# A mixture-of-experts kernel: the norms of the experts' gate and down weights taken by VectorE's maxima instead of TensorE's Gram products

## Chip, cores and metric

The kernel runs on one core of one Trainium2 chip. The metric is the device time of one execution in microseconds (us); lower is better. The median of three executions of the kernel before is 210.87 us (210.85 to 211.42).

## What is computed

For 32 sequences of 128 rows of 128 numbers, the reference adds a shared gated MLP and two of eight expert MLPs, chosen per sequence, to the input:

```
def _gemma_mlp(x, gate_w, up_w, down_w):
    g = jnp.einsum('bsh,hi->bsi', x, gate_w)
    u = jnp.einsum('bsh,hi->bsi', x, up_w)
    return jnp.einsum('bsi,ih->bsh', jax.nn.gelu(g, approximate=True) * u, down_w)
w, sel = jax.lax.top_k(softmax(router_logits), 2)
w = w / w.sum(axis=-1, keepdims=True)
...
out = out + _gemma_mlp(x, shared_gate, shared_up, shared_down)
x = x + out
```

The hidden width is 512. The weights of one kind of all eight experts are 128 x 4096 floats (2 MB).

## The kernel before

**Number format.** Only the first group of sequences is multiplied in fp32. Everything else is split: an operand is scaled by a power of two and written as a float16 high part and a float16 low part, and a product is three float16 matmuls (high by high, high by low, low by high). Each operand needs a bound of its size before it can be scaled. For x and for the shared weights VectorE takes the largest magnitude of each partition (`tops`, L379), squares it (`mask`, L393), TensorE adds the squares over the partitions with a matrix of ones (`spread_norms`, L585 and L586), and VectorE turns the exponent into scales (`scales`, L408 to L412). For the experts' weights (kinds K_GATE, K_UP and K_DOWN) TensorE multiplies each 128 x 128 block of the weights, read as bf16, with itself and adds up all 32 blocks of a kind in one PSUM tile (`gram`, L576); VectorE then keeps the diagonal (`mask`, L397), TensorE spreads it (L588), and VectorE takes the largest of it (L406) ahead of the same scales.

**Steps.** The work is 96 steps. Steps 0 to 31 are the shared MLP (8 groups of 4 sequences by 4 blocks of 128 hidden units), steps 32 to 95 the experts (32 sequences by 2). Within step t of the shared part TensorE computes the gate block G(t) (L612 to L614, output g_ps), the down block D(t - lag) of an earlier step (L625 to L627, o_ps), then the up block U(t) (L612 to L614, u_ps). The lag is 3 up to step 11, 4 up to 17, 5 up to 23, then 6; at a step where it grows there is no down block. ScalarE takes the gelu of G(t) (L335). VectorE multiplies it with U(t) into the hidden tile; this product is called H(t) below (L457). ScalarE casts H(t) to its float16 high part (L340), and GpSimd subtracts the high part from H(t) for the low part (L304), called LO(t) below. D(t) needs LO(t). G(t) and U(t) reuse two PSUM buffers each, so U(t) waits until H(t - 2) is done:

```
pe.wait_ge(gelu_ok if q == GATE else h_ok, t - 1)
```

**Side work by tables.** Every engine runs its own program in order, and tables that are keyed by step place the side work between the steps. `TOP_AT` places the maxima of x, `MASK_AT`, `SPREAD_AT` the two halves of each norm, `X_AT` the splits of x (ScalarE's high part L344, then VectorE's low part `x_low`, L418, one step later), `PIECES` the splits of the expert weights in 12 pieces of two experts (ScalarE L349, then VectorE `skill_low`, L424, one step later), `K_STEPS` the steps from which TensorE takes the Gram blocks, four steps of eight matmuls for each kind. At a step in `X_AT` or `PIECES`, GpSimd starts LO(t) only when VectorE's low part of that split is done. Group 7's first gate block, at step 28, waits for the split of x that is placed at step 23. `add_group` (L468) adds a finished group of outputs on VectorE. At the step `SKILL_TABLES_AT` GpSimd computes the scales for the expert steps, which G(32)'s gelu and H(32) wait for. Within a step VectorE's order is: H(t), `x_low` or `skill_low` of the step before, the maxima, `scales`, `mask`, `add_group`.

The Gram batch of the down weights starts with a wait for the diagonal of the up weights, since both use one PSUM tile:

```
if n == 0 and kind:
    pe.wait_ge(diag_ok, K_OF[kind - 1] + 1)
```

Of the kernel before, what the change touches and what calls it, by code (L numbers as in the profile page):

```python
# [5 lines left out]
ALU = mybir.AluOpType  # L6
ACT = mybir.ActivationFunctionType
AX = mybir.AxisListType
F32 = mybir.dt.float32
# [5 lines left out]
P = 128  # L15
# [13 lines left out]
def build(nc, xT, cond, skills, shared, outT):  # L29
    B, E = cond.shape  # L30
# [3 lines left out]
    I = W // 3  # L34
    C = I // P
    GR = 512 // S
    G = B // GR
    GN = GR * S
    assert H == P and S == P and I == GN and C == 4 and G == 8 and E == 8
    GATE, UP, DOWN = 0, 1, 2  # L40
# [7 lines left out]
    XF, XA = 2, 5  # L48
# [3 lines left out]
    with ctx:  # L52
        def sb(name, shape, dt):
            return ctx.enter_context(nc.sbuf_tensor(name, shape, dt))
# [4 lines left out]
        def sem(name):  # L59
            return ctx.enter_context(nc.semaphore(name))  # L60
# [5 lines left out]
        wsk32 = sb("wsk32", [P, 3 * E * I], F32)  # L66
# [4 lines left out]
        zeros = sb("zeros", [P, GN], BF16)  # L71
        ones = sb("ones", [P, P], BF16)
        ident = sb("ident", [P, P], F32)
        floor = sb("floor", [P, 3 + XF], BF16)
        diag = sb("diag", [P, P], BF16)


        DC, GC, UC, XC, KC = 0, 1, 2, 3, 3 + G
# [60 lines left out]
        r_wexp = sem("r_wexp")  # L139
        r_words = sem("r_words")  # L140
        top_ok = sem("top_ok")
        gram_ok = sem("gram_ok")
        diag_ok = sem("diag_ok")
        norm_ok = sem("norm_ok")
# [27 lines left out]

        FIRST, X_NEXT, K_GATE, X_REST, K_UP, K_DOWN = range(6)
        K_OF = (K_GATE, K_UP, K_DOWN)
        COLS = [(DC, XC + XF), (XC + XF, XC + XA), (KC, KC + 1), (XC + XA, XC + G), (KC + 1, KC + 2), (KC + 2, KC + 3)]


# [3 lines left out]


        TOP_AT = {1: (2,), 3: (3, 4), 10: (5,), 11: (6,), 12: (7,)}
        TOP_OF = {FIRST: 3 + XF, X_NEXT: 3 + XA, X_REST: 3 + G}
        K_STEPS = [5, 10, 15]
        MASK_AT = {3: X_NEXT, 9: K_GATE, 12: X_REST, 14: K_UP, 19: K_DOWN}
        SPREAD_AT = {4: X_NEXT, 11: K_GATE, 14: X_REST, 16: K_UP, 21: K_DOWN}
        ROUTE_AT = 6
        ROUTED_AT = 11

        TABLE_AT = {4: X_NEXT, 15: X_REST}
        SKILL_TABLES_AT = 23


        X_AT = {3: 0, 5: 2, 8: 3, 11: 4, 15: 5, 19: 6, 23: 7}
        X_NTH = {1: 1} | {j: n + 2 for n, j in enumerate(X_AT.values())}
        EG = 2
        PIECES = {12 + 2 * n: n for n in range(3 * E // EG)}


        def lag(t):
# [175 lines left out]
        def _(dve):  # L377
# [7 lines left out]
            def top_x(j):  # L385
                dve.wait_ge(x_in[0 if j == 0 else 1 if j < XF else 2 if j < XA else 3], 16)
                tops(XC + j, xT32[:, j * GN:(j + 1) * GN])

            def mask(n):
                a, b = COLS[n]  # L390
                if n not in K_OF:
                    dve.wait_ge(top_ok, TOP_OF[n])
                    nc.vector.tensor_tensor(top2[:, a:b], top[:, a:b], top[:, a:b], ALU.mult).then_inc(diag_ok, 1)  # L393
                else:
                    kind = K_OF.index(n)
                    dve.wait_ge(gram_ok, kind + 1)
                    nc.vector.scalar_tensor_tensor(out=diag[:, :], in0=n_ps[0][:, 0:P], scalar=NORM_FLOOR,  # L397
                                                   in1=ident[:, :], op0=ALU.add, op1=ALU.mult).then_inc(diag_ok, 1)

            def scales(n):  # L400
                a, b = COLS[n]
                dve.wait_ge(norm_ok, n + 1)
                norm = n_ps[1][:, 0:b - a]
                if n in K_OF:
                    norm = n_all[:, a:b]
                    nc.vector.tensor_reduce(norm, n_ps[1][:, 0:P], AX.X, ALU.max).then_inc(n_red, 1)  # L406
                    dve.wait_ge(n_red, K_OF.index(n) + 1)
                nc.vector.tensor_scalar(e_bits[:, a:b], norm.bitcast(U32), 1, EXP_MASK,  # L408
                                        ALU.logical_shift_right, ALU.bitwise_and).then_inc(s_step, 1)
                dve.wait_ge(s_step, n + 1)  # L410
                nc.vector.tensor_scalar(i_bits[:, a:b], e_bits[:, a:b], 1.0, INV_FIELD * ONE_EXP, ALU.mult, ALU.add)
                nc.vector.tensor_scalar(s_bits[:, a:b], e_bits[:, a:b], -1.0, SCALE_FIELD * ONE_EXP,  # L412
                                        ALU.mult, ALU.add).then_inc(scaled, 1)
                dve.wait_ge(scaled, n + 1)
# [111 lines left out]
            for t in range(STEPS):  # L526
                hidden(t)

                if t - 1 in X_AT:
                    x_low(X_AT[t - 1])  # L530
                if t - 1 in PIECES:
                    skill_low(PIECES[t - 1])
                if t == 0:
                    scales(FIRST)
                if t in TOP_AT:
                    for j in TOP_AT[t]:
                        top_x(j)
                if t == 2:
                    shared_low(GATE, 1)
                    x_low(1)  # L540
                    shared_low(UP, 2)
                if t == C:
                    shared_low(DOWN, 3)
                if t in SPREAD_AT:
                    scales(SPREAD_AT[t])
                if t in MASK_AT:
                    mask(MASK_AT[t])
                if t == C - 1:
                    routing_weights()
                    routing_spread()  # L550
                if t == ROUTED_AT:
                    routed_tables()

                if t == 7:
                    add_group(0)
                n, c = divmod(down_of(t - 1), C)
                if c == C - 1 and 1 <= n < G and down_of(t - 1) != down_of(t - 2):
                    add_group(n)
                b, k = divmod(t - SH - LAG - 1, TOP_K)
                if k == TOP_K - 1 and b >= 0:  # L560
                    add_row(b)
# [4 lines left out]
        def _(pe):  # L566
# [4 lines left out]
            def gram(out, src, start):  # L571

                n = src.shape[1] // P
                for i in range(n):
                    block_ap = high_bits(src[:, i * P:(i + 1) * P])
                    last = nc.tensor.matmul(out, block_ap, block_ap, start=(start and i == 0), stop=(i == n - 1),  # L576
                                            skip_group_check=True)
                return last

            def spread_norms(n):  # L580
                a, b = COLS[n]
                pe.wait_ge(diag_ok, n + 1)
                if n not in K_OF:
                    sums = n_ps[1][:, 0:b - a]
                    nc.tensor.matmul(sums, ones[:, :], floor[:, 0:b - a], start=True, stop=False)  # L585
                    nc.tensor.matmul(sums, ones[:, :], top2[:, a:b], start=False, stop=True).then_inc(norm_ok, 1)  # L586
                else:
                    nc.tensor.matmul(n_ps[1][:, 0:P], ones[:, :], diag[:, :], start=True, stop=True).then_inc(norm_ok, 1)  # L588
# [95 lines left out]
            for t in range(2, SH):  # L684
                if t >= C:
                    half_shared(t, GATE)
                    if down_of(t) >= C and down_of(t) != down_of(t - 1):
                        down_shared(down_of(t))

                    if t - C < 2:  # L690
                        down_first(t - 2)
                    if t in SPREAD_AT:
                        spread_norms(SPREAD_AT[t])
                    half_shared(t, UP)
                elif t == C - 1:
                    gate_up_first(t, GATE)
                    gate_up_first(t, UP)
                    down_first(1)
                for kind in range(3):
                    n = t - K_STEPS[kind]  # L700
                    if 0 <= n < 4:
                        if n == 0:
                            pe.wait_ge(sk_in[kind], 16)
                        if n == 0 and kind:
                            pe.wait_ge(diag_ok, K_OF[kind - 1] + 1)
                        a = (kind * E + 2 * n) * I
                        for half in range(2):
                            last = gram(n_ps[0][:, 0:P], wsk32[:, a + half * I:a + (half + 1) * I],
                                        n == 0 and half == 0)
                        if n == 3:  # L710
                            last.then_inc(gram_ok, 1)
                if t == ROUTE_AT:
                    pe.wait_ge(r_spread, 2 * TOP_K)
                    pe.wait_ge(s_step, X_NEXT + 1)
                    nc.tensor.matmul(n_ps[1][:, P:P + 2 * TOP_K * B], ones32[:, :], spread[:, :, :].rearrange("p b q -> p (b q)"),
                                     start=True, stop=True).then_inc(r_routed, 1)
# [73 lines left out]
```

## Time and profile before

| | |
|---|---|
| median of three executions | 210.87 us |
| the profiled execution, its own time | 211.93 us |
| its span in the trace | 210.1 us |
| granted TensorE clock | full in every stretch |
| TensorE busy | 205.2 us of the span |
| VectorE, ScalarE, GpSimd busy | 123.6, 133.8, 117.9 us |

The span is the time from the first to the last instruction in the trace. The profiled execution's own time is 1.8 us longer than its span, and 1.06 us longer than the median of the three. The work of each engine is read from a list of its instructions in order of time; an instruction of a row starts when the one ahead of it on that engine lets it, which for VectorE is a little before the recorded end of that one.

### The profile page before, as it was taken

The numbers are of one execution on the slowest core, as the hardware profiler recorded it, in microseconds if no ns is written. First come the engines' busy times: TensorE is split into PE (matmuls) and PEld (weight loads), VectorE is DVE, ScalarE is ACT, GpSimd is POOL, SyncE is SP. The second block draws the span as 40 slices with busy tenths as digits, with TensorE's granted clock in tenths as the row PEclk, the third lists the DMA queues.
The fourth block names the chain that finished last, engine by engine and source line by source line (L and its number), as shares of the span: only waits on it lengthen the run. The fifth ranks groups of instructions, "written<-read, shape, count | busy, mean of one in ns | idle before, by whom it ended". The sixth has DMA issues, their size and how long they took to land.

```text
span 210.1 us, 6672 instructions
## 1 busy us (share of the span) xinstructions
PE 205.2 (98%) x2695; PEld 165.0 (79%) x2695; DVE 123.6 (59%) x217; ACT 133.8 (64%) x217; POOL 117.9 (56%) x129
## 2 busy tenths in 40 slices
PE   7999999989999999999999999999999999999995
PEld 2444555445444478899999999999999999999995
DVE  2899657977999988554353444434435435344452
ACT  6283767677989997655656656556565565655650
POOL 3023644359548997665565655655656556565562
PEclk9999999999999999999999999999999999999999
DMA  6999600000000000000010010010010010010011
GB/s 196 391 433 434 296 2 0 0 3 0 2 0 5 0 0 3 0 3 5 3 53 3 0 53 3 3 53 0 3 55 3 3 53 0 3 53 4 3 50 53
DMA packets 2813, 11.70 MB, mean 56 GB/s; under 512 B 352, under 2 KB 608, under 8 KB 2400
## 3 DMA queue, kind: packets, MB, share of 16 engines
q1 hardware_dynamic: 2640, 11.01, 13.1%
q8 instruction: 23, 0.38, 0.7%
q10 hardware_dynamic: 144, 0.26, 0.7%
q14 instruction: 6, 0.05, 0.1%
HBM read 9.18 MB, written 2.10 MB: 54 GB/s over the span
## 4 chain that ended last, share of the span: by engine, by line
PE 93%; DVE 4%; issue 1%; ACT 0%; POOL 0%; POOLq 0%
PE o_ps L664 7%; PE g_ps L646 7%; PE u_ps L646 7%; PE o_ps L663 7%; PE u_ps L645 7%; PE g_ps L645 7%; PE u_ps L644 7%; PE g_ps L644 7%; PE o_ps L662 7%; PE u_ps L612 3%; PE g_ps L612 3%; PE g_ps L614 2%; PE o_ps L627 2%; PE o_ps L625 2%; PE o_ps L626 2%; PE g_ps L613 2%
## 5 line engine op out<-in xcount | busy, mean ns | idle before, releaser
L304 POOL TENSOR_TENSOR h<-h 128x512 f16<-128x512 f32 x92 | 109.2, 1194 | 79.2 <-ACT h L340 57.9
L457 DVE SCALAR_TENSOR_TENSOR h<-gel,sk_factor,u_ps 128x512 f32<-128x512 f32 x64 | 47.8, 747 | 68.0 <-PE u_ps L646 39.0
L335 ACT ACTIVATE gel<-g_ps,sk_gate 128x512 f32<-128x512 f32 x64 | 43.9, 687 | 49.8 <-PE g_ps L646 49.8
L340 ACT CAST h<-h 128x512 f16<-128x512 f32 x92 | 56.0, 609 | 3.5 <-DVE h L457 3.5
L645 PE MATMUL g_ps<-x,wsk 128*128 128x128 f16 x256 | 46.2, 219 | 0.0
L646 PE MATMUL g_ps<-x,wsk 128*128 128x128 f16 x256 | 46.2, 219 | 0.0
L645 PE MATMUL u_ps<-x,wsk 128*128 128x128 f16 x256 | 46.2, 219 | 0.0
L646 PE MATMUL u_ps<-x,wsk 128*128 128x128 f16 x256 | 46.2, 219 | 0.0
L644 PE MATMUL u_ps<-x,wsk 128*128 128x128 f16 x256 | 46.2, 219 | 0.0
L644 PE MATMUL g_ps<-x,wsk 128*128 128x128 f16 x256 | 46.2, 219 | 0.0
L663 PE MATMUL o_ps<-h,wsk 128*128 128x128 f16 x256 | 45.9, 219 | 0.0
L664 PE MATMUL o_ps<-h,wsk 128*128 128x128 f16 x256 | 45.9, 219 | 0.0
L662 PE MATMUL o_ps<-h,wsk 128*128 128x128 f16 x256 | 45.9, 219 | 0.0
L457 DVE SCALAR_TENSOR_TENSOR h<-gel,sh_factor,u_ps 128x512 f32<-128x512 f32 x28 | 20.7, 741 | 8.6 <-ACT gel L335 4.3
L645 PEld LDWEIGHTS u_ps<-x,wsk 128*128 x256 | 25.0, 98 | 0.7
L644 PEld LDWEIGHTS u_ps<-x,wsk 128*128 x256 | 25.1, 98 | 0.7
L335 ACT ACTIVATE gel<-g_ps,sh_gate 128x512 f32<-128x512 f32 x28 | 19.1, 681 | 10.1 <-PE g_ps L614 9.9
L645 PEld LDWEIGHTS g_ps<-x,wsk 128*128 x256 | 25.0, 98 | 0.1
L644 PEld LDWEIGHTS g_ps<-x,wsk 128*128 x256 | 25.0, 98 | 0.1
L646 PEld LDWEIGHTS g_ps<-x,wsk 128*128 x256 | 25.1, 98 | 0.0
L664 PEld LDWEIGHTS o_ps<-h,wsk 128*128 x256 | 25.0, 98 | 0.0
L646 PEld LDWEIGHTS u_ps<-x,wsk 128*128 x256 | 25.0, 98 | 0.0
(103 smaller groups left out, 310.1 us busy)
## 6 DMA issues: line engine op xcount, KB each, us to landing
wsk<-skills SPq DMA_DIRECT2D x3, 2048.0 KB, 16.1
outT<-xT SPq DMA_DIRECT2D x7, 256.0 KB, 2.0
xT<-xT SPq DMA_DIRECT2D x2, 768.0 KB, 6.3
wsh<-shared SPq DMA_DIRECT2D x3, 256.0 KB, 3.9
xT<-xT ACTq DMA_DIRECT2D x1, 256.0 KB, 3.5
xT<-xT SPq DMA_DIRECT2D x1, 256.0 KB, 4.6
outT<-xT SPq DMA_DIRECT2D x1, 192.0 KB, 2.6
outT<-xT SPq DMA_DIRECT2D x1, 64.0 KB, 1.5
```

What stands on the lines that cost most here:

```text
L304: nc.gpsimd.tensor_tensor(hidden_lo(t), hidden_full(t), hidden_hi(t), ALU.subtract).then_inc(lo_ok, 1)
L335: nc.scalar.activation(gel[:, t % NG, :], g_ps[t % 2][:, :], ACT.Gelu_apprx_tanh, scale=scale).then_inc(gelu_ok, 1)
L340: nc.scalar.copy(hidden_hi(t), hidden_full(t)).then_inc(hi_ok, 1)
L457: nc.vector.scalar_tensor_tensor(out=h32[:, t % N32, :], in0=gel[:, t % NG, :], scalar=factor, in1=u_ps[t % 2][:, :], op0=ALU.mult, op1=AL ...
L612: nc.tensor.matmul(out, w_hi, xh, start=True, stop=False)
L613: nc.tensor.matmul(out, w_hi, xl, start=False, stop=False)
L644: nc.tensor.matmul(cols, w_hi[c], xh, start=True, stop=False)
L645: nc.tensor.matmul(cols, w_hi[c], xl, start=False, stop=False)
L646: last = nc.tensor.matmul(cols, w_lo[c], xh, start=False, stop=True)
L662: nc.tensor.matmul(out, w_hi[c], hi, start=(k == 0 and c == 0), stop=False)
L663: nc.tensor.matmul(out, w_hi[c], lo, start=False, stop=False)
L664: last = nc.tensor.matmul(out, w_lo[c], hi, start=False, stop=(k == TOP_K - 1 and c == C - 1))
```

## The change

The Gram product stays for the up weights alone (`GRAMS`) and runs at steps 9 to 12 instead of 10 to 13. For the gate and the down weights VectorE takes the largest magnitude of each partition over two experts at a time (`part_top`: 128 x 1024 floats to 128 x 1), four times for each kind, at steps 5, 6, 7, 8 and 17, 19, 21, 23. It then reduces the four to one and goes the way of x: square, sum over the partitions with the matrix of ones, scales. The tables move: gate's norm is ready a step earlier, down's 6 steps later; the splits of the last four groups of x come one step later; the splits of the gate and up weights come one step earlier; those of the down weights stay where they were; GpSimd's tables for the experts come at step 28 instead of 23.

```
+        GRAMS = (K_UP,)
...
-        TOP_OF = {FIRST: 3 + XF, X_NEXT: 3 + XA, X_REST: 3 + G}
-        K_STEPS = [5, 10, 15]
-        MASK_AT = {3: X_NEXT, 9: K_GATE, 12: X_REST, 14: K_UP, 19: K_DOWN}
-        SPREAD_AT = {4: X_NEXT, 11: K_GATE, 14: X_REST, 16: K_UP, 21: K_DOWN}
+        TOP_OF = {FIRST: 3 + XF, X_NEXT: 3 + XA, X_REST: 4 + G, K_GATE: 4 + XA, K_DOWN: 5 + G}
+        PART_AT = {5: (GATE, 0), 6: (GATE, 1), 7: (GATE, 2), 8: (GATE, 3), 17: (DOWN, 0), 19: (DOWN, 1), 21: (DOWN, 2), 23: (DOWN, 3)}
+        K_STEPS = {K_UP: 9}
+        MASK_AT = {3: X_NEXT, 8: K_GATE, 12: X_REST, 14: K_UP, 24: K_DOWN}
+        SPREAD_AT = {4: X_NEXT, 10: K_GATE, 14: X_REST, 16: K_UP, 27: K_DOWN}
...
-        SKILL_TABLES_AT = 23
-        X_AT = {3: 0, 5: 2, 8: 3, 11: 4, 15: 5, 19: 6, 23: 7}
+        SKILL_TABLES_AT = 28
+        X_AT = {3: 0, 5: 2, 8: 3, 12: 4, 16: 5, 20: 6, 24: 7}
...
-        PIECES = {12 + 2 * n: n for n in range(3 * E // EG)}
+        PIECES = {t: n for n, t in enumerate((11, 13, 15, 17, 19, 21, 23, 25, 28, 30, 32, 34))}
...
+            def part_top(kind, n):
+                if n == 0:
+                    dve.wait_ge(sk_in[kind], 16)
+                nc.vector.tensor_reduce(parts[:, kind // 2, n:n + 1], wsk32[:, (kind * E + 2 * n) * I:(kind * E + 2 * n + 2) * I],
+                                        AX.X, ALU.max, apply_absolute_value=True).then_inc(part_ok, 1)
+
             def mask(n):
                 a, b = COLS[n]
-                if n not in K_OF:
+                if n in K_OF and n not in GRAMS:
+                    kind = K_OF.index(n)
+                    dve.wait_ge(part_ok, E // 2 if kind == GATE else E)
+                    tops(KC + kind, parts[:, kind // 2, :])
+                if n not in GRAMS:
                     dve.wait_ge(top_ok, TOP_OF[n])
                     nc.vector.tensor_tensor(top2[:, a:b], top[:, a:b], top[:, a:b], ALU.mult).then_inc(diag_ok, 1)
...
+                if t in PART_AT:
+                    part_top(*PART_AT[t])
...
-                if n not in K_OF:
+                if n not in GRAMS:
                     sums = n_ps[1][:, 0:b - a]
...
-                for kind in range(3):
-                    n = t - K_STEPS[kind]
+                for batch in GRAMS:
+                    kind = K_OF.index(batch)
+                    n = t - K_STEPS[batch]
...
-                        if n == 0 and kind:
-                            pe.wait_ge(diag_ok, K_OF[kind - 1] + 1)
```

TensorE around steps 5 to 7, before (output and inputs by name; g_ps0 and u_ps0 belong to even steps):

```order
L614 MATMUL u_ps1<-x2,wsh 128x512
L576 MATMUL n_ps0<-wsk32 128x128 x8
L612 MATMUL g_ps0<-x2,wsh 128x512
L613 MATMUL g_ps0<-x2,wsh 128x512
L614 MATMUL g_ps0<-x2,wsh 128x512
L612 MATMUL u_ps0<-x2,wsh 128x512
L613 MATMUL u_ps0<-x2,wsh 128x512
L614 MATMUL u_ps0<-x2,wsh 128x512
L576 MATMUL n_ps0<-wsk32 128x128 x8
L715 MATMUL n_ps1<-spread,ones32 128x128
```

and with the change, the same place:

```order
L629 MATMUL u_ps1<-x2,wsh 128x512
L627 MATMUL g_ps0<-x2,wsh 128x512
L628 MATMUL g_ps0<-x2,wsh 128x512
L629 MATMUL g_ps0<-x2,wsh 128x512
L627 MATMUL u_ps0<-x2,wsh 128x512
L628 MATMUL u_ps0<-x2,wsh 128x512
L629 MATMUL u_ps0<-x2,wsh 128x512
L728 MATMUL n_ps1<-spread,ones32 128x128
```

The eight Gram matmuls of each step are gone here, and so at seven other places, less the up batch, which moves one step forward.

VectorE from H(23) to H(27), before (h32 is the hidden tile, wsk a weight split, x2 a split of x, xT32 an added group):

```order
L457 SCALAR_TENSOR_TENSOR h32<-gel,sh_factor,u_ps1 128x512
L424 SCALAR_TENSOR_TENSOR wsk<-wsk32,s_bits,wsk 128x1024
L457 SCALAR_TENSOR_TENSOR h32<-gel,sh_factor,u_ps0 128x512
L418 SCALAR_TENSOR_TENSOR x2<-xT32,s_bits,x2 128x4x128
L457 SCALAR_TENSOR_TENSOR h32<-gel,sh_factor,u_ps1 128x512
L424 SCALAR_TENSOR_TENSOR wsk<-wsk32,s_bits,wsk 128x1024
L457 SCALAR_TENSOR_TENSOR h32<-gel,sh_factor,u_ps0 128x512
L468 SCALAR_TENSOR_TENSOR xT32<-o_ps0,sh_inv,xT32 128x512
L457 SCALAR_TENSOR_TENSOR h32<-gel,sh_factor,u_ps1 128x512
```

and with the change, the same five products:

```order
L470 SCALAR_TENSOR_TENSOR h32<-gel,sh_factor,u_ps1 128x512
L396 TENSOR_REDUCE parts<-wsk32 128x1
L470 SCALAR_TENSOR_TENSOR h32<-gel,sh_factor,u_ps0 128x512
L437 SCALAR_TENSOR_TENSOR wsk<-wsk32,s_bits,wsk 128x1024
L383 TENSOR_REDUCE top<-parts 128x1
L407 TENSOR_TENSOR top2<-top 128x1
L470 SCALAR_TENSOR_TENSOR h32<-gel,sh_factor,u_ps1 128x512
L431 SCALAR_TENSOR_TENSOR x2<-xT32,s_bits,x2 128x4x128
L470 SCALAR_TENSOR_TENSOR h32<-gel,sh_factor,u_ps0 128x512
L437 SCALAR_TENSOR_TENSOR wsk<-wsk32,s_bits,wsk 128x1024
L481 SCALAR_TENSOR_TENSOR xT32<-o_ps0,sh_inv,xT32 128x512
L470 SCALAR_TENSOR_TENSOR h32<-gel,sh_factor,u_ps1 128x512
```

A maximum over two experts and down's first half of the norm have come in, each weight split stands a step earlier, and the split of x a step later.

## Rows read from the trace of the kernel before

**Rows 1.** The page: busy time; the chain that ended last.
```profile
PE 205.2 (98%) x2695; PEld 165.0 (79%) x2695; DVE 123.6 (59%) x217; ACT 133.8 (64%) x217; POOL 117.9 (56%) x129
...
PE 93%; DVE 4%; issue 1%; ACT 0%; POOL 0%; POOLq 0%
```

**Rows 2.** Windows: us, then busy us and instruction count per engine, granted clock, DMA.
```profile
20.88:36.83 15.95, 15.95 (x111) 8.59 (x110) 10.40 (x22) 11.34 (x19) 7.95 (x10) 1.00 0.24 103
36.83:48.72 11.89, 10.72 (x76) 5.59 (x74) 10.67 (x21) 8.61 (x13) 5.78 (x6) 1.00 0.01 1
48.72:60.05 11.33, 11.33 (x61) 5.40 (x59) 9.87 (x17) 9.98 (x15) 7.70 (x10) 1.00 0.00 1
60.05:72.09 12.04, 12.04 (x57) 5.30 (x56) 11.21 (x14) 10.86 (x17) 9.35 (x12) 1.00 0.01 2
```

**Rows 3.** TensorE in order of time: start, us, work, idle before it.
```profile
31.85 0.38 PE L625 MATMUL o_ps<-h,wsh 128*128 128x512 f16 x1
...
34.95 0.62 PE L576 MATMUL n_ps<-wsk 128*128 128x128 bf16 x8
35.42 0.38 PE L612 MATMUL g_ps<-x,wsh 128*128 128x512 f16 x1
...
39.60 0.18 PE L585 MATMUL n_ps<-floor,ones 128*128 128x3 bf16 x1 [0.33 <-DVE top L393]
...
43.26 0.62 PE L576 MATMUL n_ps<-wsk 128*128 128x128 bf16 x8 [0.84 <-DVE diag L397]
...
60.84 0.39 PE L612 MATMUL u_ps<-x,wsh 128*128 128x512 f16 x1
...
67.33 0.38 PE L612 MATMUL g_ps<-x,wsh 128*128 128x512 f16 x1
...
70.57 0.38 PE L612 MATMUL u_ps<-x,wsh 128*128 128x512 f16 x1
```

**Rows 4.** VectorE in order of time, same columns.
```profile
14.83 1.27 DVE L379 TENSOR_REDUCE top<-xT 128x1 f32<-128x512 f32 x2
...
20.88 0.75 DVE L457 SCALAR_TENSOR_TENSOR h<-gel,sh_factor,u_ps 128x512 f32<-128x512 f32 x1
...
29.66 0.75 DVE L418 SCALAR_TENSOR_TENSOR x<-xT,s_bits,x 128x512 f16<-128x512 f32 x1
...
33.46 0.75 DVE L457 SCALAR_TENSOR_TENSOR h<-gel,sh_factor,u_ps 128x512 f32<-128x512 f32 x1 [1.18 <-ACT gel L335]
34.12 0.68 DVE L379 TENSOR_REDUCE top<-xT 128x1 f32<-128x512 f32 x1
...
40.12 1.27 DVE L424 SCALAR_TENSOR_TENSOR wsk<-wsk,s_bits 128x1024 f16<-128x1024 f32 x1
41.32 0.73 DVE L457 SCALAR_TENSOR_TENSOR h<-gel,sh_factor,u_ps 128x512 f32<-128x512 f32 x1
41.98 0.15 DVE L408 TENSOR_SCALAR e_bits<-n_ps 128x3 uint32<-128x3 uint32 x1
42.16 0.56 DVE L411 TENSOR_SCALAR i_bits<-e_bits 128x3 int32<-128x3 uint32 x1
...
45.97 0.75 DVE L457 SCALAR_TENSOR_TENSOR h<-gel,sh_factor,u_ps 128x512 f32<-128x512 f32 x1 [1.01 <-ACT gel L335]
...
60.05 1.40 DVE L457 SCALAR_TENSOR_TENSOR h<-gel,sh_factor,u_ps 128x512 f32<-128x512 f32 x2
...
68.11 0.73 DVE L457 SCALAR_TENSOR_TENSOR h<-gel,sh_factor,u_ps 128x512 f32<-128x512 f32 x1
68.77 2.17 DVE L424 SCALAR_TENSOR_TENSOR wsk<-wsk,s_bits 128x1024 f16<-128x1024 f32 x1
```

**Rows 5.** GpSimd in order of time, same columns.
```profile
30.55 2.27 POOL L304 TENSOR_TENSOR h<-h 128x512 f16<-128x512 f32 x2 [2.83 <-DVE x L418]
33.32 1.16 POOL L304 TENSOR_TENSOR h<-h 128x512 f16<-128x512 f32 x1 [0.50 <-ACT h L340]
...
41.54 2.27 POOL L304 TENSOR_TENSOR h<-h 128x512 f16<-128x512 f32 x2 [2.02 <-DVE wsk L424]
...
65.78 1.24 POOL L284 TENSOR_SCALAR tmp_k<-s_bits 128x8 f32<-128x8 f32 x1
...
68.70 11.94 POOL L304 TENSOR_TENSOR h<-h 128x512 f16<-128x512 f32 x8
```

More of the change, by code:

```diff
@@ L73, in build @@
         ident = sb("ident", [P, P], F32)
+        parts = sb("parts", [P, 2, E // 2], F32)
         floor = sb("floor", [P, 3 + XF], BF16)
@@ L141, in build @@
         top_ok = sem("top_ok")
+        part_ok = sem("part_ok")
         gram_ok = sem("gram_ok")
@@ L394, in mask @@
                 else:
-                    kind = K_OF.index(n)
-                    dve.wait_ge(gram_ok, kind + 1)
+                    dve.wait_ge(gram_ok, GRAMS.index(n) + 1)
                     nc.vector.scalar_tensor_tensor(out=diag[:, :], in0=n_ps[0][:, 0:P], scalar=NORM_FLOOR,
@@ L403, in scales @@
                 norm = n_ps[1][:, 0:b - a]
-                if n in K_OF:
+                if n in GRAMS:
                     norm = n_all[:, a:b]
                     nc.vector.tensor_reduce(norm, n_ps[1][:, 0:P], AX.X, ALU.max).then_inc(n_red, 1)
-                    dve.wait_ge(n_red, K_OF.index(n) + 1)
+                    dve.wait_ge(n_red, GRAMS.index(n) + 1)
                 nc.vector.tensor_scalar(e_bits[:, a:b], norm.bitcast(U32), 1, EXP_MASK,
@@ L703, in _ @@
                             pe.wait_ge(sk_in[kind], 16)
-                        if n == 0 and kind:
-                            pe.wait_ge(diag_ok, K_OF[kind - 1] + 1)
                         a = (kind * E + 2 * n) * I
                         for half in range(2):
-                            last = gram(n_ps[0][:, 0:P], wsk32[:, a + half * I:a + (half + 1) * I],
-                                        n == 0 and half == 0)
+                            last = gram(n_ps[0][:, 0:P], wsk32[:, a + half * I:a + (half + 1) * I], n == 0 and half == 0)
                         if n == 3:
```

## The prediction

> **What bounds the kernel now.** I read the page first. TensorE is busy 205.2 us of a 210.1 us span, and 93% of the chain that ended last is TensorE's own instructions [rows 1]. That says little about this change, because it moves work only between about 20 and 75 us, and the other engines are near their limit there. So the windows come second: VectorE is busy for 10.40 of 15.95 us from H(5) to H(12), 10.67 of 11.89 us from H(12) to H(17), 9.87 of 11.33 us up to H(22), and 11.21 of 12.04 us up to H(29) [rows 2]. TensorE is busy throughout except in the second window, where it stands for 0.33 us and 0.84 us, both times for VectorE [rows 3]. The reader should see two engines almost level. Freeing TensorE brings time only as far as VectorE, which gets the work, lets it run ahead.
>
> A difference under 0.3%, 0.63 us, is one that a measurement of this kernel can't tell from none.
>
> **What TensorE loses.** A group of eight Gram matmuls takes 0.47 us, from 34.95 to the gate block at 35.42 [rows 3]. Eight such groups go, four of the gate weights and four of the down weights: 8 x 0.47 = 3.8 us. The wait of 0.84 us at 43.26 [rows 3] goes with the down batch. The two small matmuls that spread a diagonal become pairs of as small ones, nothing. If TensorE alone decided, the span would fall by 3.8 + 0.84 = 4.6 us.
>
> **What VectorE gains.** No row shows a maximum over 1024 floats. The nearest rows bound it. Two maxima over 512 end 1.27 us after the first starts, one alone is 0.68 us, so one starts 0.59 to 0.60 us after another [rows 4]. Twice that, 1.20 us, is the upper bound. For the lower one: a split of 1024 floats takes 1.20 us from start to start (40.12 to 41.32) and a product over 512 takes 0.66 us (41.32 to 41.98) [rows 4], so 512 floats more cost 0.54 us and the rest is fixed: 0.60 + 0.54 = 1.14 us. Both kinds run on the same engine, so I take 1.13 us, at the lower bound. Eight make 9.0 us. The small instructions (reduce four values, square) are worth what leaves (diagonal, largest of it), 0.4 us either way.
>
> **The port.** Some VectorE instructions stop for a running GpSimd one: the split at 68.77 takes 2.17 us instead of 1.27, beside a GpSimd subtraction that starts at 68.70 [rows 4, 5], and the small scale instruction at 42.16 takes 0.56 us, until the first of two GpSimd subtractions that start at 41.54 is over [rows 4, 5]. The price is up to what is left of one subtraction, 2.27 / 2 = 1.14 us. Products and maxima aren't hit: the maximum at 34.12 takes 0.68 us beside the subtraction that starts at 33.32 [rows 4, 5]. So the eight new maxima wait for nobody. The Trainium skill ("SBUF — State Buffer", Who interferes with whom) says the same of tensor_reduce on this chip, and that of two instructions that contend the one that issues second is blocked for the whole of the other. If maxima did contend, the four of the down weights could each cost up to 1.14 us more, 4.6 us in all, and the sum below would be 5.3 instead of 0.7; the trace speaks against that.
>
> **Walk through the steps.** VectorE's row starts at 20.88 for H(5), as before. Every chain of VectorE's below takes 0.66 us for a product, an x split or an added group.
>
> *Steps 5 to 11.* Five products, two groups of other 0.66 us (x split, added group), four maxima at 1.13 and gate's first half, 0.45 us, are 3.30 + 1.32 + 4.52 + 0.45 = 9.6 us, so the split of group 3 starts at 30.5 instead of 29.66 [rows 4]. VectorE stood idle here for much of the time (10.40 of 15.95 us busy [rows 2]); that cover is used up. LO(8) is held for this split: before it started at 30.55, 0.89 us after the split's start, and the down block that needs it at 31.85 [rows 3, 5]. Now it starts at 31.3 and takes 1.14 us, and the down block starts at about 32.6. TensorE, which did 1.9 us less Gram work in steps 5 to 8 but 0.47 us more at step 9, is 0.7 us late, and H(11) starts at 34.15 instead of 33.46 [rows 4].
>
> *Steps 11 to 16.* The first two weight splits come here in both kernels. The square of x's maxima at step 12 runs into LO(11), 0.65 us, and the second split into LO(12), 0.6 us. But TensorE has no wait of 0.84 us and no Gram work at steps 13, 15 and 16. VectorE's chain reaches the up diagonal at 44.1, U(16) follows at 44.5 and H(16) at 45.4 instead of 45.97 [rows 4]: now 0.6 us early.
>
> *Steps 16 to 22.* VectorE is the bound. Before, this stretch took 60.05 - 45.97 = 14.1 us [rows 4], with some 1.2 us of it idle. Three maxima come in (3.4 us), the down norm leaves (0.95 us), and port waits stay about as long: 14.1 - 1.2 + 3.4 - 0.95 - 0.6 (product by product) = 14.75 us. H(22) starts at 60.15 instead of 60.05. U(24) needs it: it started 0.79 us after H(22), at 60.84 [rows 3], and now starts at 60.95. By that step TensorE has nothing left of its gain: it stands there for 2 us.
>
> *Steps 22 to 27.* H(22) to H(26), 3.3 us; three weight splits where there were two, since they stand a step earlier, 3.6; the x split, 0.66; the last maximum, 1.13; the down norm's first half, 0.4; the added group, 0.66; port waits for x split and third weight split, 0.65. Sum 10.4 us, against 68.11 - 60.05 = 8.06 [rows 4]. H(27) starts at 70.5 instead of 68.11. U(29) needs it 0.79 us later, at 71.3; before it ran at 70.57 and had 1.7 us of slack [rows 3]. That is **+0.7 us**. The x split of group 7, a step later, ends at 67.6 and lets G(28) start at 67.75 instead of 67.33 [rows 3]: +0.4, inside the other.
>
> *After step 27.* VectorE is free of maxima, TensorE runs on its own work as before, and nothing gives the 0.7 us back. GpSimd's tables for the experts take 2.9 us (65.78 to 68.70 [rows 5]). They come after LO(28), which waits for the first down split, at about 75, so end near 79. The gelu of step 32 would want them at about 77.3. U(34) and G(34) are what wait for it, two steps of 2 us on, so I cost the move at nothing.
>
> Sum: -4.6 us of TensorE's, of which nothing is left at step 24, and +0.7 us of VectorE's at step 29. On the profiled execution's 211.93 us that gives 212.6 us; its time stands 1.06 us above the median of 210.87, so the median becomes **211.6 us**.
>
> **Rivals.** *The port falls worse at step 14.* The scales of x's last groups follow the second weight split directly, and LO(13) is held for that same split. Before, a product lay between (41.32 [rows 4]). If GpSimd starts first, the scale instruction waits the 1.14 us. It delays the up diagonal, which TensorE waits for in front of U(16), and everything behind. VectorE's instruction would come about 0.03 us earlier by the pace of the rows, too close to call. Price +1.1: median 212.7. The Trainium skill ("SBUF — State Buffer", Who interferes with whom) says that the order of issue alone decides which of the two is blocked.
>
> *TensorE keeps a part of its gain (faster).* The place is the x split of group 7 in front of G(28), and H(27) behind it. My walk has port waits of 1.25 us between H(11) and H(16) and 0.65 us from there to that split. If 1.15 us of these 1.9 don't fall, and as much before H(27), G(28) starts at 66.6 instead of 67.33 and U(29) with it: -0.7 us, median 210.15. It starts to be faster at all from 0.42 us less of VectorE time ahead of that split, and can be measured from 1.05 us less. For it speaks that my port waits are estimates from the overlap of two engines whose phase shifts; against it, that a wait of 0.9 us for the port did fall in the kernel before (68.77 [rows 4]).
>
> *GpSimd late.* If LO(28) and the tables slip beyond about 80.5, gelu(32) holds G(34), and the expert steps start late: for each us that the chain is later than in my walk, up to one us. With the 11.94 us of eight subtractions in a row [rows 5] GpSimd had hardly any slack in that stretch. Price +2: median 212.9 to 213.5.
>
> *The change not doing what it says* is out: the order of instructions shows the Gram groups gone and the maxima in place. The data moved are the same, and the norm's value changes no duration.
>
> **How the numbers follow.** My case has a chance of 0.42, with an own range of 210.7 to 212.3 (maxima of 1.20 instead of 1.13 add 0.3, port waits of half or one and a half times my count -0.6 or +0.6); of it 0.02 lies under -0.63 us, 0.18 within, 0.22 above. The port at step 14 has 0.25, all slower. The faster rival has 0.20, of which 0.16 is faster and 0.04 within. GpSimd late has 0.07, slower. A cancelling of these effects near zero has 0.06. Together: faster 0.18, same 0.28, slower 0.54. The range for 8 in 10 reaches from the faster rival's 210.0 to the late tables' 213.1.
>
> **What would show it.** Right: the maxima at 1.13 to 1.20 us; H(11) at about 34.2, U(16) at 44.5, a wait of TensorE of some 2 us for H(22) in front of U(24), H(27) at 70.5, and TensorE without a wait from step 30 on. Wrong: TensorE waits of under 1 us in all between 45 and 72 us, or H(27) before 69.7, which would make it faster; a wait of a gelu for GpSimd's tables that reaches TensorE.

## The result and the profile after

The changed kernel takes 214.37 us (median of four, 213.95 to 214.71) against 210.90 us before: a ratio of **1.0151, 95% interval 1.0132 to 1.0171**. The forecast was slower by 0.7 us, 211.6 us, in a range of 210.0 to 213.1 us. The kernel is slower by 3.2 us by the ratio (3.5 us between the two medians), and its time lies outside that range. The direction was right, the size was not. In the three later series the kernel before had medians of 211.5 to 211.7 us, so a part of the gap may be that its first four executions were short ones.

The spans of the two profiled executions differ by only 2.1 us (212.2 and 210.1). The start hides a part of the difference: up to H(5), where both programs still do the same, the execution before took 20.88 us and the one after 20.04 us, since the first transfers and matmuls fall a little differently in each execution (19.66 to 21.50 us over all kernels of this study). So I compare from the start of H(5) to the start of VectorE's last instruction. Before that is 207.82 - 20.88 = 186.94 us, after it is 209.85 - 20.04 = 189.81 us: **+2.87 us**. Below, "length" means this number, and a time behind a plus sign is measured from H(5).

The page of the changed kernel, busy time of the engines, answers to [rows 1]:

```profile
PE 201.9 (95%) x2633; PEld 160.3 (76%) x2633; DVE 131.3 (62%) x225; ACT 133.9 (63%) x217; POOL 114.5 (54%) x129
```

TensorE is busy 3.3 us less and VectorE 7.7 us more. Now the windows from H(5) to H(11), to H(16), to H(22) and to H(27), first before, then after (us, busy us and instructions of TensorE, its weight loads, VectorE, ScalarE, GpSimd, clock, DMA):

```profile
20.88:33.46 12.58, 12.58 (x87) 6.67 (x86) 7.20 (x11) 8.61 (x15) 6.92 (x10) 1.00 0.31 131
33.46:45.97 12.51, 11.34 (x81) 5.89 (x79) 11.23 (x24) 9.31 (x15) 5.31 (x5) 1.00 0.00 1
45.97:60.05 14.08, 14.08 (x84) 7.04 (x82) 12.51 (x23) 12.01 (x18) 9.20 (x12) 1.00 0.00 1
60.05:68.11 8.06, 8.06 (x38) 3.52 (x37) 7.72 (x10) 7.29 (x12) 5.43 (x7) 1.00 0.01 3
```

```profile
20.04:33.38 13.34, 11.73 (x72) 5.58 (x72) 11.78 (x19) 9.22 (x15) 7.30 (x10) 1.00 0.35 149
33.38:45.60 12.22, 10.32 (x60) 4.73 (x58) 11.68 (x20) 8.90 (x14) 5.22 (x5) 1.00 0.00 0
45.60:60.47 14.87, 13.84 (x63) 5.77 (x61) 14.76 (x21) 11.99 (x19) 8.32 (x10) 1.00 0.01 2
60.47:70.85 10.38, 9.52 (x46) 4.20 (x47) 10.35 (x15) 8.38 (x13) 5.04 (x5) 1.00 0.00 1
```

Before, TensorE is busy for every microsecond of three of the four windows. After, it has idle time in all four, and VectorE is busy for 14.76 of 14.87 us and 10.35 of 10.38 us in the last two. The bound has moved from TensorE to VectorE. VectorE's rows in order of time, answering to [rows 4]:

```profile
20.70 1.21 DVE L396 TENSOR_REDUCE parts<-wsk 128x1 f32<-128x1024 f32 x1
21.83 0.74 DVE L470 SCALAR_TENSOR_TENSOR h<-gel,sh_factor,u_ps 128x512 f32<-128x512 f32 x1
...
33.38 0.75 DVE L470 SCALAR_TENSOR_TENSOR h<-gel,sh_factor,u_ps 128x512 f32<-128x512 f32 x1 [1.18 <-PE u_ps L629]
...
41.13 1.80 DVE L437 SCALAR_TENSOR_TENSOR wsk<-wsk,s_bits 128x1024 f16<-128x1024 f32 x1
42.85 0.15 DVE L421 TENSOR_SCALAR e_bits<-n_ps 128x3 uint32<-128x3 uint32 x1
43.04 0.17 DVE L424 TENSOR_SCALAR i_bits<-e_bits 128x3 int32<-128x3 uint32 x1
43.12 1.13 DVE L425 TENSOR_SCALAR s_bits<-e_bits 128x3 int32<-128x3 uint32 x1
44.28 0.29 DVE L410 SCALAR_TENSOR_TENSOR diag<-n_ps,ident 128x128 bf16<-128x128 f32 x1
...
70.85 0.73 DVE L470 SCALAR_TENSOR_TENSOR h<-gel,sh_factor,u_ps 128x512 f32<-128x512 f32 x1
```

A maximum takes 1.21 us and the next product starts 1.13 us after it. The scales are three small instructions; the second and the third take their values from SBUF, and these two are meant below. The GpSimd subtraction that the split at 41.13 releases starts between them:

```profile
43.07 2.27 POOL L308 TENSOR_TENSOR h<-h 128x512 f16<-128x512 f32 x2 [1.22 <-DVE wsk L437]
```

The first of the two slips in at 43.04, the second one, at 43.12, stands for 1.13 us; the up diagonal comes at 44.28. From the start of this instruction to the diagonal it is 1.16 us, against 0.19 us where the port is free (42.63 to 42.82 in the kernel before), so the stop delays the diagonal by 0.97 us. The three longest waits of TensorE behind step 14, answering to [rows 3]:

```profile
44.63 0.23 PE L603 MATMUL n_ps<-diag,ones 128*128 128x128 bf16 x1 [1.24 <-DVE diag L410]
...
61.26 0.39 PE L627 MATMUL u_ps<-x,wsh 128*128 128x512 f16 x1 [1.55 <-DVE h L470]
...
80.94 0.23 PE L659 MATMUL g_ps<-x,wsk 128*128 128x128 f16 x1 [0.62 <-ACT gel L339]
```

They are the spreading of the up norm and U(16) behind the up diagonal, U(24) behind H(22), and G(34) behind the gelu of step 32. What that gelu waited for stands in ScalarE's and GpSimd's rows (compare [rows 5]):

```profile
75.97 1.16 POOL L308 TENSOR_TENSOR h<-h 128x512 f16<-128x512 f32 x1 [2.18 <-DVE wsk L437]
...
79.87 0.29 POOL L296 TENSOR_TENSOR sk_factor<-tmp_k,wexp 128x64 f32<-128x64 f32 x1
```

```profile
80.20 0.69 ACT L339 ACTIVATE gel<-g_ps,sk_gate 128x512 f32<-128x512 f32 x1 [2.61 <-POOL sk_factor L296]
```

LO(28) waits for the first down split, the tables come behind it, and the gelu stands 2.61 us for them.

### The profile page after: what moved, and what is told of

The parts are those of the page before. It is cut to its first block, busy times and chain, and to the rows that moved or that the text cites. A ratio compares the mean times of both kernels' runs of the same rounds, so it can differ in the third digit from the quotient of the medians.

```text
span 212.2 us, 6554 instructions
## 1 busy us (share of the span) xinstructions
PE 201.9 (95%) x2633; PEld 160.3 (76%) x2633; DVE 131.3 (62%) x225; ACT 133.9 (63%) x217; POOL 114.5 (54%) x129
## 2 busy tenths in 40 slices
DMA packets 2812, 11.68 MB, mean 55 GB/s; under 512 B 352, under 2 KB 608, under 8 KB 2400
## 4 chain that ended last, share of the span: by engine, by line
PE 64%; DVE 3%; POOL 2%; ACT 1%; issue 0%; DVEq 0%; POOLq 0%
PE o_ps L679 7%; PE o_ps L678 7%; PE o_ps L677 7%; PE g_ps L659 7%; PE g_ps L661 7%; PE u_ps L661 7%; PE u_ps L660 7%; PE g_ps L660 7%; PE u_ps L659 7%; DVE wsk L437 1%; DVE h L470 1%; PE o_ps L642 1%; PE o_ps L640 1%; PE o_ps L641 1%; POOL sk_gate L290 1%; ACT gel L339 1%
## 5 line engine op out<-in xcount | busy, mean ns | idle before, releaser
L308 POOL TENSOR_TENSOR h<-h 128x512 f16<-128x512 f32 x92 | 106.3, 1162 | 85.3 <-ACT h L344 61.6
L678 PEld LDWEIGHTS o_ps<-h,wsk 128*128 x256 | 25.0, 98 | 0.0
L677 PEld LDWEIGHTS o_ps<-h,wsk 128*128 x256 | 25.0, 98 | 0.0
L679 PEld LDWEIGHTS o_ps<-h,wsk 128*128 x256 | 25.0, 98 | 0.0
```

What stands on the lines that cost most here:

```text
L308: nc.gpsimd.tensor_tensor(hidden_lo(t), hidden_full(t), hidden_hi(t), ALU.subtract).then_inc(lo_ok, 1)
L677: nc.tensor.matmul(out, w_hi[c], hi, start=(k == 0 and c == 0), stop=False)
L678: nc.tensor.matmul(out, w_hi[c], lo, start=False, stop=False)
L679: last = nc.tensor.matmul(out, w_lo[c], hi, start=False, stop=(k == TOP_K - 1 and c == C - 1))
```

## The experiments

Ratios are against the kernel before, timed beside each kernel on the same chip; lengths are from one profile each.

**Tables at step 27.**

```
-        SKILL_TABLES_AT = 28
+        SKILL_TABLES_AT = 27
```

> The changed kernel with GpSimd's expert tables at step 27 instead of 28, so that they no longer queue behind LO(28), which waits for a weight split. Theory A (three delays one behind the other: VectorE's longer chain, the port at step 14, the late tables): gelu(32) no longer waits for the tables and G(34) starts 0.8 us earlier, ratio to the kernel before about 1.0115 instead of 1.0151, about 213.5 us. Theory B (VectorE's maxima alone make the loss, the table wait is covered): 214.4 us, ratio 1.015.

Measured: 1.0095 (1.0070 to 1.0121), length 188.87 us, 0.94 us less. The wait of gelu(32) for the tables is gone. Theory A holds, and the late tables alone cost 0.9 us. (At step 27 the tables stand ahead of LO(28), so they no longer wait for the first down split.)

**Second weight split at step 14.**

```
-        PIECES = {... (11, 13, 15, 17, ...
+        PIECES = {... (11, 14, 15, 17, ...
```

> The changed kernel with the second weight split moved from step 13 to 14, so that the scales of x's last groups no longer stand between that split and the GpSimd subtraction it releases. Theory A: the up diagonal is ready 1 to 2 us earlier, U(16) too, H(16) 0.2 to 1.2 us earlier (VectorE's work is the same), and the end 0.2 to 1.2 us earlier: 213.2 to 214.2 us. Theory B: the sum of VectorE's work decides, the order does not: 214.4 us.

Measured: 1.0085 (1.0068 to 1.0103), length 188.81 us, 1.00 us less. H(16) starts at + 24.31 us instead of + 25.56 us. VectorE has the same instructions in another order:

```profile
41.25 0.15 DVE L421 TENSOR_SCALAR e_bits<-n_ps 128x3 uint32<-128x3 uint32 x1
41.43 0.57 DVE L424 TENSOR_SCALAR i_bits<-e_bits 128x3 int32<-128x3 uint32 x1
41.91 0.15 DVE L425 TENSOR_SCALAR s_bits<-e_bits 128x3 int32<-128x3 uint32 x1
42.10 0.29 DVE L410 SCALAR_TENSOR_TENSOR diag<-n_ps,ident 128x128 bf16<-128x128 f32 x1
...
42.98 1.28 DVE L437 SCALAR_TENSOR_TENSOR wsk<-wsk,s_bits 128x1024 f16<-128x1024 f32 x1
```

The scales still meet a subtraction of GpSimd's, but the diagonal stands ahead of the split, at + 21.96 us instead of + 24.24 us, and TensorE's wait in front of U(16) goes. The edit does two things at once: it takes the long stop out of the scales, and it moves the split, 1.72 us from start to start in the changed kernel, behind the diagonal. That order decides and not the sum of VectorE's work is shown; how much of the 1.00 us is the port alone is not. The rows of the changed kernel give the port 0.97 us of the diagonal's delay.

**Each half of the change alone.** First gate's maxima in the kernel before; the tables, and with them the places of all splits, are those of before.

```
-        K_STEPS = [5, 10, 15]
+        GRAMS = (K_UP, K_DOWN)
+        K_STEPS = {K_UP: 10, K_DOWN: 15}
+        PART_AT = {5: (GATE, 0), 6: (GATE, 1), 7: (GATE, 2), 8: (GATE, 3)}
```

> The kernel before with only the gate weights' norm by VectorE's maxima at steps 5 to 8 (all tables as before, Gram products for up and down). Theory A: H(11) is 0.7 us late, but VectorE has 1.0 to 1.5 us of idle time behind it and TensorE 1.9 us less to do: between 210.2 and 211.3 us, ratio 0.997 to 1.002. Theory B (a maximum costs its time wherever it stands) and theory C (the delay of step 8's split starts it all): 212 to 213 us, ratio 1.006 to 1.01.

Measured: 1.0012 (1.0001 to 1.0023), length 186.91 us against 186.94. H(11) starts at + 12.86 us (before + 12.58) and H(16) at + 25.06 us (before + 25.09). Theories B and C fall: exchanging gate's Gram products for maxima costs nothing on balance here, and it brings nothing either.

Then the down maxima alone:

```
+        GRAMS = (K_GATE, K_UP)
+        PART_AT = {17: (DOWN, 0), 19: (DOWN, 1), 21: (DOWN, 2), 23: (DOWN, 3)}
-        MASK_AT = {..., 19: K_DOWN}
-        SPREAD_AT = {..., 21: K_DOWN}
-        SKILL_TABLES_AT = 23
+        MASK_AT = {..., 24: K_DOWN}
+        SPREAD_AT = {..., 27: K_DOWN}
+        SKILL_TABLES_AT = 28
```

> The kernel before with only the down weights' norm by VectorE's maxima at steps 17 to 23, first half of the norm at 24, second at 27, tables at 28 (else all as before, Gram products for gate and up). Theory A: VectorE's chain from H(16) to H(27) grows by about 2.4 us of which 1.7 is slack, and the late tables come on top: 212.3 to 213.3 us, ratio 1.007 to 1.011. Theory C (gate's maxima do it): 210.9 us, ratio 1.000.

Measured: 1.0077 (1.0056 to 1.0098), length 188.39 us, +1.45 us, with gelu(32)'s wait of 2.6 us for the tables in it. So the two halves alone make about 1.4 of the 2.87 us, all of it in the down half. The other 1.4 us shows in neither: it comes only with the moved tables and both halves together. The second weight split at step 13 is 1.00 us of it; the rest, about 0.4 us, was not taken apart.

**Both repairs.** The changed kernel with the edits of the first two experiments.

> The changed kernel with both repairs: the second weight split at step 14, GpSimd's tables at step 27. If the three delays lie one behind the other, the two gains add up: 1.0151 - 0.0056 - 0.0066 = 1.003 against the kernel before. If they cover each other, 1.008 as with one of them. What is left is VectorE's chain up to H(27).

Measured: 1.0033 (1.0012 to 1.0053), length 187.86 us, 0.92 us more than before. The two gains add up: 0.94 + 1.00 = 1.94 us, and 189.81 - 187.86 = 1.95 us. So these two delays lie one behind the other and do not cover each other.

**The down maxima made short.** In the kernel with both repairs:

```
-  wsk32[:, (kind * E + 2 * n) * I:(kind * E + 2 * n + 2) * I]
+  wsk32[:, (kind * E + 2 * n) * I:(kind * E + 2 * n) * I + (32 if kind == DOWN else 2 * I)]
```

> As e5_both, but each of the down weights' four maxima reads 32 floats of a partition instead of 1024 (it leaves out the rest, so the bound is taken over a part of the weights); order and waits are the same. If VectorE's time for the down maxima is what holds the kernel: 4.2 us less of VectorE ahead of H(27), TensorE becomes the bound again and ends 2 to 2.7 us earlier, ratio 0.990 to 0.993. If the loss lay in the order or in later scales: 1.003 as e5_both.

Measured: 0.9943 (0.9923 to 0.9964), length 185.97 us. It is 1.89 us less than with whole maxima, under the 2 to 2.7 us expected but far from none, so VectorE's time for them is what holds this kernel. But four maxima of 0.18 us instead of 1.21 us free 4.1 us, and less than half of it shows. VectorE's rows tell why:

```profile
50.18 0.18 DVE L396 TENSOR_REDUCE parts<-wsk 128x1 f32<-128x32 f32 x1
50.27 0.74 DVE L470 SCALAR_TENSOR_TENSOR h<-gel,sh_factor,u_ps 128x512 f32<-128x512 f32 x1
50.93 1.72 DVE L437 SCALAR_TENSOR_TENSOR wsk<-wsk,s_bits 128x1024 f16<-128x1024 f32 x1
...
54.04 2.10 DVE L437 SCALAR_TENSOR_TENSOR wsk<-wsk,s_bits 128x1024 f16<-128x1024 f32 x1
...
62.38 1.72 DVE L437 SCALAR_TENSOR_TENSOR wsk<-wsk,s_bits 128x1024 f16<-128x1024 f32 x1
```

These three weight splits take 1.72, 2.10 and 1.72 us instead of 1.28, 1.28 and 1.27 with whole maxima: earlier by a maximum, they now run into GpSimd's subtractions. That is 1.7 of the 2.2 us that do not show. With whole maxima GpSimd had time to finish. From H(16) to H(22) both engines are now nearly full (VectorE busy for 13.27, TensorE for 13.33 of 13.37 us); behind that TensorE still waits 0.48 us for H(22), so it is not the bound throughout, as had been expected.

**The gate maxima made short.** The kernel with gate's maxima alone, each over 32 floats.

> As e3_gate_alone, but each of the gate weights' four maxima reads 32 floats of a partition instead of 1024 (the rest is left out). If gate's maxima at steps 5 to 8 give back what TensorE gains by making the split of group 3 and H(11) late, this kernel is 1.2 to 1.9 us faster than the kernel before, ratio 0.991 to 0.995. If VectorE's work behind H(11) decides alone, 1.000 as e3_gate_alone.

Measured: 0.9959 (0.9936 to 0.9981), length 186.12 us, 0.79 us less than with whole maxima. So the gate Gram products are worth 0.82 us where the maxima take next to no time, and whole maxima take nearly all of it back. That is less than the 1.2 to 1.9 us expected. Even with maxima this short TensorE stands for a split of x, for LO(5), and later for the up diagonal:

```profile
23.49 0.38 PE L627 MATMUL g_ps<-x,wsh 128*128 128x512 f16 x1 [0.59 <-DVE x L431]
24.70 0.39 PE L640 MATMUL o_ps<-h,wsh 128*128 128x512 f16 x1 [0.41 <-POOL h L308]
...
42.16 0.62 PE L591 MATMUL n_ps<-wsk 128*128 128x128 bf16 x8 [0.85 <-DVE diag L410]
```

**Towards a faster kernel.** VectorE is nearly full from H(12) on and has room at steps 6 to 8. In the kernel before:

```
-        TOP_AT = {1: (2,), 3: (3, 4), 10: (5,), 11: (6,), 12: (7,)}
+        TOP_AT = {1: (2,), 3: (3, 4), 6: (5,), 7: (6,), 8: (7,)}
-        SPREAD_AT = {..., 14: X_REST, ...
+        SPREAD_AT = {..., 13: X_REST, ...
```

> The kernel before with the maxima of x's last three groups at steps 6, 7 and 8, where VectorE idles, instead of 10, 11 and 12, and TensorE's half of their norm at step 13 instead of 14; all else as before. It takes 0.6 us and a port wait out of VectorE's full stretch from H(12) on. If that stretch holds TensorE (its waits of 0.33 and 0.84 us), the end is 0.8 to 1.2 us earlier, ratio 0.994 to 0.996. If not, 1.000.

Measured: 0.9995 (0.9978 to 1.0012), length 186.80 us: a miss. With the norm's second half at step 13 the scales stand right behind a weight split, as in the changed kernel, and stop for the port, behind a GpSimd subtraction that starts at 41.43:

```profile
40.00 1.28 DVE L424 SCALAR_TENSOR_TENSOR wsk<-wsk,s_bits 128x1024 f16<-128x1024 f32 x1
41.20 0.15 DVE L408 TENSOR_SCALAR e_bits<-n_ps 128x3 uint32<-128x3 uint32 x1
41.39 0.17 DVE L411 TENSOR_SCALAR i_bits<-e_bits 128x3 int32<-128x3 uint32 x1
41.47 1.14 DVE L412 TENSOR_SCALAR s_bits<-e_bits 128x3 int32<-128x3 uint32 x1
```

With `TOP_AT` alone changed:

> As e8, but TensorE's half of the norm of x's last groups stays at step 14. In e8 the scales of these groups came right behind a weight split and waited 1.14 us for a GpSimd subtraction; here a product lies between again. If that wait took e8's gain: 0.8 to 1.1 us from H(5) to the end less than before, ratio 0.995 to 0.996. If maxima at 10 to 12 never held TensorE: 1.000.

Measured: 0.9957 (0.9934 to 0.9979), length 185.57 us. One table entry, 13 or 14, is worth 1.2 us of length (0.8 us by the ratios). The number came as expected, but its cause is another than the expectation names. At step 13 TensorE comes to its half of the norm before VectorE has taken the square, and stands; at step 14 it does not. First the kernel with the entry 13, then the one with 14:

```profile
38.37 0.18 PE L585 MATMUL n_ps<-floor,ones 128*128 128x3 bf16 x1 [0.89 <-DVE top L393]
```

```profile
39.14 0.17 PE L585 MATMUL n_ps<-floor,ones 128*128 128x3 bf16 x1
```

This is 3.1 us ahead of the stop for the port, and H(13) is by then 1.09 us later than with the entry 14 (+ 17.84 against + 16.75). TensorE's starts tell what each stand costs, since one matmul follows another by 0.22 us where nothing stops it. The stand at step 13 costs 1.04 us. The port's stop reaches TensorE only through the up diagonal, in front of the down batch: 0.31 us against 0.13 us with the entry 14. The kernel before loses 0.49 and 1.00 us in its two waits, 1.49 us in all. These sums, 1.35, 0.13 and 1.49 us, give the differences of the three lengths (186.80, 185.57, 186.94) to 0.02 us. So early maxima gain because TensorE's two waits go, and the entry 13 puts in a new one; by these rows the port has at most 0.3 us of the miss.

The Gram batch of the down weights one step later, in the kernel before:

```
-        K_STEPS = [5, 10, 15]
-        MASK_AT = {..., 19: K_DOWN}
-        SPREAD_AT = {..., 16: K_UP, 21: K_DOWN}
+        K_STEPS = [5, 10, 16]
+        MASK_AT = {..., 20: K_DOWN}
+        SPREAD_AT = {..., 17: K_UP, 22: K_DOWN}
```

> The kernel before with the Gram batch of the down weights one step later (16 to 19), its norm and the spreading of the up norm one step later too. TensorE no longer stands 0.84 us for the up diagonal at step 15. If that wait alone is worth its length: 0.8 us less, ratio 0.996. If VectorE's chain behind it holds H(17) and later ones anyway: 0 to 0.3 us, ratio 0.999 to 1.000.

Measured: 0.9950 (0.9927 to 0.9972), length 185.83 us. TensorE's wait of 0.84 us, 1.00 us from start to start, is gone, and the end comes 1.1 us earlier. VectorE's chain behind it takes nothing back.

Both edits:

> e9 and e10 together. TensorE's waits of 0.33 and 0.84 us are both gone and VectorE has 1.2 us less ahead of H(16): 1.0 to 1.2 us less, ratio 0.9945 to 0.995. If VectorE's chain of steps 16 to 22 takes over: about 0.5 us, ratio 0.9975.

Measured: 0.9926 (0.9895 to 0.9957), length 185.33 us. This has the lowest ratio of the study, 0.7% under the kernel before, with all norms by Gram products; its interval overlaps with those of the two single edits. The gains do not add up (1.37 and 1.11 us alone, 1.61 us together), and can't, since the early maxima alone already take away both of TensorE's waits. From H(5) at 20.20 us to 62 us TensorE is busy for 41.80 of 41.80 us, and its own work is the bound.

Gate's maxima with the later Gram batch:

> e3_gate_alone (gate's norm by maxima) with the down weights' Gram batch one step later as in e10. If gate's maxima gave nothing because TensorE's spared 1.9 us ended in its waits at steps 8 and 15, the second of 0.85 us now goes: ratio 0.996 to 0.998. If VectorE's chain from H(11) on holds all: 1.001 as e3.

Measured: 0.9950 (0.9932 to 0.9967), length 185.79 us, as without gate's maxima (185.83 us). The idea that TensorE's spared time ended in the wait at step 15 is wrong: the later batch gains as much with Gram products at steps 5 to 8 as without. The spared time ends earlier. Up to 62 us TensorE is busy 1.40 us less than without gate's maxima (40.11 against 41.51 us) and stands 1.70 instead of 0.32 us, first for the split of x that VectorE makes at step 6:

```profile
23.54 0.38 PE L627 MATMUL g_ps<-x,wsh 128*128 128x512 f16 x1 [1.04 <-DVE x L431]
24.75 0.39 PE L640 MATMUL o_ps<-h,wsh 128*128 128x512 f16 x1 [0.41 <-POOL h L308]
```

## Why the prediction was right or wrong

The forecast was 2.8 us too low (211.6 against 214.37 us). Two steps of it failed: the order at the port at step 14, which the walk took the good way, and the late tables for GpSimd, which it cost at nothing. A third error, in the range, was to treat them as cases that exclude each other.

- **What TensorE loses**: right in the main. It is busy 3.3 us less (3.8 expected), and none of it reaches the end. The wait of 0.84 us went with the down batch, but one of 1.24 us came in front of U(16).
- **A maximum of 1.13 us from start to start**: right, to 0.01 us. That maxima don't wait for the port: right, all eight take 1.21 us, also the one at 50.21, beside a subtraction that starts at 50.43.
- **Steps 5 to 11**: right. H(11) came at + 13.34 us; the walk said 34.15 - 20.88 = + 13.27. The down block behind LO(8) came at + 11.68 us (walk: + 11.7), but waits only 0.17 us: most of what TensorE had gained was gone before, in waits of 1.04 us for a split of x and 0.41 us for LO(5), which the walk does not have.
- **Steps 11 to 16**: wrong by 1.0 us. The walk said + 24.5 us for H(16), it was + 25.56. The step that failed is the choice between the two orders at the port: I let both scale instructions through ahead of GpSimd. The first did pass, by the 0.03 us that the rival names (43.04 against 43.07), the second stood 1.13 us. The diagonal came at + 24.24 us instead of 44.1 - 20.88 = + 23.2. The rival "the port falls worse at step 14" held, and its price of 1.1 us fits; moving one split gave 1.00 us back at the end, though that edit also puts the split behind the diagonal.
- **Steps 16 to 22 and 22 to 27**: right, 14.87 and 10.38 us against 14.75 and 10.35. TensorE waited 1.55 us in front of U(24), where I said 2 us. With both repairs the kernel is 0.92 us longer than before; my walk said 0.7 us.
- **After step 27, "so I cost the move at nothing"**: wrong by 0.94 us. The tables ended at 80.16, + 60.1 us; the walk had them near 79, + 58.1. LO(28) started at + 55.9 and not at + 54.1: 1.0 us of that came from step 14 and 0.8 us from elsewhere (with the split at step 14 it starts at + 54.9). The subtraction and the tables themselves took 0.15 us more than I had. The point from which this reaches TensorE was misplaced too: I put it at 80.5, + 59.6. With both repairs G(34) runs undelayed at 80.02, + 59.1 us, and its gelu takes 0.69 us, so the tables had to be done by + 58.4. The margin was 0.3 us, not 1.5, and I called it nothing. This slack was the term that was mis-sized. So even without the delay of step 14 the late tables cost 0.95 us (188.81 against 187.86). The rival "GpSimd late" held in its mechanism; its price of 2 us was too high.
- **How the numbers follow**: this is where the size went. The delays lie one behind the other on one chain: each of the two repairs gains the same alone and with the other. What is left with both, 0.92 us, and the 1.00 and 0.95 us that they give back make the 2.87 us of the profiles (that this sum comes out follows from how the terms are taken; that the gains don't depend on each other is what was measured). I gave the two rivals chances of their own as if they excluded my case and each other, and gave the range no case in which both held. It should have reached at least 0.7 + 1.1 + 0.9 = 2.7 us, 213.6 us, and further with the errors of each.
- **The faster rival** had no part. Port waits did not ease by themselves; where the down maxima were made short, they grew.

## What to carry to other kernels

Where two engines are almost level, work taken from one and given to the other pays only up to the first wait for the other; here eight groups of Gram products less, 3.3 us of TensorE's busy time, bought nothing, and two moves in the tables, which took away TensorE's two waits for VectorE, gained 0.7% in its stead. Add the delays of a chain, do not choose between them: a cost that you can't place and a slack of a few tenths belong into the sum together. When an instruction's end releases a neighbour that shares a port, look at what its own engine does next. And when a time comes out as forecast, look for the waits of the engine that is the bound before you call the cause shown: here the stop for the port was the expected cause of a miss, and a wait of TensorE's 3 us earlier was the real one.

## What the runs showed of the hardware

Two small scale instructions on 128 x 3 values, right behind the split that releases GpSimd, behaved alike in the changed kernel and in the kernel with early maxima of x and the entry 13: the first started 0.03 and 0.04 us ahead of the subtraction and took 0.17 us, the second started 0.05 and 0.04 us behind its start and took 1.13 and 1.14 us, the length of a GpSimd subtraction. The Trainium skill ("SBUF — State Buffer", Who interferes with whom) says that the one that issues second is blocked for the whole of the other; the rows agree. I had expected a toss; it fell the same way both times, between the two instructions. And freeing 4.1 us of VectorE brought 1.9 us, since three of its splits then took 1.72, 2.10 and 1.72 us instead of 1.28: here the wait for the port depended on phase, and the maxima, which take 1.21 us beside a subtraction too, had served as a gap for GpSimd.
